# Gated expert tiles computed in turned form with biases as columns and their outputs scattered by token, and an opening without its own barrier

## What is computed

```python
D, H, E, K = 128, 342, 8, 2
d2 = sum(xs*xs) + sum(centroid*centroid) - 2 * xs @ centroid.T
w, sel = top_k(sqrt(max(d2, 1e-12)), K);  w = softmax(w)
for e in range(E):
    h = silu(xs @ Wg[e] + bg[e]) * (xs @ W1[e] + b1[e])
    out = out + we[:, e:e+1] * (h @ W2[e] + b2[e])
```

## Time and profile before

| | us |
|---|---|
| runs | 2288.75, 2294.0, 2300.62 (median 2294.0) |
| profiled execution, its own time | 2291.14 |
| its span | 2289.4 |
| PE busy in the span | 1860.5 (81%) |
| DVE, ACT, POOL busy | 1044.9, 846.4, 639.2 |
| mean granted TensorE clock | 0.887 |

### The profile page before, as it was taken

One profiled execution on the slowest core, in us unless ns is written; L12 is line 12 of the kernel. 1 busy time (PEld: TensorE's weight loads), 2 busy tenths in 40 slices (PEclk: granted clock), 3 DMA queues, 4 the chain that ended last, 5 costly groups with the idle time before them and its releaser, 6 DMA issues.

```text
span 2289.4 us, 47265 instructions
## 1 busy us (share of the span) xinstructions
PE 1860.5 (81%) x18716; PEld 1258.7 (55%) x18716; DVE 1044.9 (46%) x2763; ACT 846.4 (37%) x2360; POOL 639.2 (28%) x637
## 2 busy tenths in 40 slices
PE   3999984785699999799996029999207999999988
PEld 1555563664587788555555015555104666666773
DVE  4566556665421212356555102222234555555558
ACT  1333321664244444233332002222103555555636
POOL 4122103675110111212210560000571333333315
PEclk8999976887699999899997559999658999999979
DMA  4000000000000000200002140000111000000001
GB/s 150 12 12 7 2 1 23 19 6 5 1 1 2 2 1 1 88 12 12 7 2 86 39 117 19 19 20 19 39 43 53 6 6 6 6 6 1 1 1 38
DMA packets 47940, 51.11 MB, mean 22 GB/s; under 512 B 8025, under 2 KB 38633, under 8 KB 47465
## 3 DMA queue, kind: packets, MB, share of 16 engines
q1 hardware_dynamic: 43628, 39.64, 5.6%
q0 software_dynamic: 4096, 8.40, 1.3%
HBM read 32.25 MB, written 15.77 MB: 21 GB/s over the span
## 4 chain that ended last, share of the span: by engine, by line
PE 57%; issue 9%; POOL 9%; DVE 5%; POOLq 4%; DMA 1%; ACT 1%; DVEq 1%; SPq 0%; ACTq 0%
PE single L1471 5%; PE quad L1459 5%; PE quad L1783 4%; PE pair L362 3%; PE single L1802 3%; POOL arena L2034 3%; POOL tokens_by_tile L2024 3%; PE single L413 2%; PE quad L390 2%; PE pair L2190 2%; PE quad L2190 1%; PE pair L1418 1%; PE single L2202 1%; PE quad L2167 1%; PE quad L2216 1%
## 5 line engine op out<-in xcount | busy, mean ns | idle before, releaser
L531 DVE TENSOR_REDUCE arena<-pair 128x8 f32<-128x1024 f32 x128 | 156.8, 1225 | 156.5 <-PE pair L362 154.1
L2423 POOL TENSOR_TENSOR arena<-arena 128x512 f32<-128x512 f32 x128 | 130.4, 1040 | 310.3 <-DVE arena L2346 310.3
L613 POOL TENSOR_SCALAR arena<-arena 128x512 f32<-128x512 f32 x56 | 86.7, 1565 | 330.3 <-ACT arena L467 330.3
L1971 DVE TENSOR_TENSOR arena<-quad,arena 128x342 f32<-128x342 f32 x72 | 37.1, 515 | 273.7 <-ACT arena L1840 171.2
L238 POOL TENSOR_TENSOR rstd<-var_eps,neg_half 128x4 f32<-128x4 f32 (+1 forms) x64 | 65.6, 1024 | 333.5 <-DVE var_eps L234 237.8
L513 ACT ACTIVATE arena<-quad 128x1024 f32<-128x1024 f32 x128 | 124.2, 1022 | 69.5 <-PE quad L396 69.5
L1529 ACT ACTIVATE arena<-quad,arena 128x256 f32<-128x256 f32 x256 | 110.8, 475 | 101.8 <-PE quad L1459 101.8
L362 PE MATMUL pair<-arena 32*128 32x512 f32 x512 | 147.4, 653 | 0.0
L2034 POOL DMA_INDIRECT arena<-outputs_by_tile,arena x64 | 61.5, 960 | 277.0 <-DMA outputs_by_tile<-arena 258.5
L1459 PE MATMUL quad<-arena,wide 128*128 128x256 f32 x512 | 123.3, 389 | 4.6 <-issue 3.8
L2283 ACT ACTIVATE arena<-pair,arena 128x128 f32<-128x128 f32 x256 | 90.9, 380 | 90.7 <-DVE arena L2341 90.7
(11 more groups left out here) (475 smaller groups left out, 4410.6 us busy)
## 6 DMA issues: line engine op xcount, KB each, us to landing
arena<-in_ctxT SPq DMA_DIRECT2D x32, 256.0 KB, 2.8
tokens_by_tile<-arena SPq DMA_DIRECT2D x8, 576.0 KB, 6.6
arena<-tokens_by_tile SPq DMA_DIRECT2D x8, 576.0 KB, 7.7
outputs_by_tile<-arena SPq DMA_DIRECT2D x72, 64.0 KB, 1.5
wide<-in_w SPq DMA_DIRECT2D x2, 2048.0 KB, 9.7
wide<-in_wgu SPq DMA_DIRECT2D x1, 2736.0 KB
x<-in_x SPq DMA_DIRECT2D x4, 512.0 KB, 6.0
out_x<-x SPq DMA_DIRECT2D x8, 256.0 KB, 2.3
```

What stands on the lines that cost most here:

```text
L531: dve.tensor_reduce(mx[m % 2][:, 8 * p:8 * p + 8], S[:].rearrange("p (h k) -> p h k", h=8), AX.X, ALU.max).then_inc(s["s_free"], 1)
L613: mm = pool.tensor_scalar(kv[g % 2][:, :, a, :], kf[g % 2], kmask[:, a:a + 1], None, ALU.mult)
L2423: pool.tensor_tensor(part, part, inv[t % 3][:, 4 * r:4 * r + 4].unsqueeze(2).broadcast_to([P, 4, P]), ALU.mult).then_inc(s["norm_ready"], 1)
```

## The change

**Opening.** The load phase has no barrier. SP issues x part 0, the eight loads of the first attention, the first two context tiles, and then the rest. DVE computes the statistics of two groups, and those of group g+2 inside the attention at its batch 4g. POOL computes only the constants that this attention needs (`consts_in`), takes `rstd` group by group (`setup_r`), and makes the causal mask and `earlier` at g = 2. The masks of layer 2 are made by DVE at batch 7.

**Routing.** A row of the token table has 130 words: the token, its number, and its first choice. The row indices are ready before the list of experts by tile. The three-way split of the biases, its DRAM trip and its broadcast are gone; six small products with a one-hot list give `bcols`, the biases as columns for each tile. `W2` has a 115th row with its bias, which meets a row of ones in `hidT`.

**Tiles.** ACT copies the tile's 684 columns of weights from `wide` to `wt` (`copy_weights`), picked by a register of its own. PE uses pieces of 114 columns of `wt` as the stationary operand and the turned tokens as the moving one, so that the hidden layer comes out turned and needs no transposes. Silu takes the bias column on ACT, three pieces; DVE adds the other bias and multiplies, three pieces. DVE copies the turned tokens and the result. POOL scatters each tile's result to its token's row of `outputs_by_choice`, with an index list that DVE computes every 9 tiles (`places`); rows of padding have an index beyond the bound and are skipped.

**End.** SP waits for the last stores and loads two blocks of 256 KB per group, ACT scales them (8 instructions per group), POOL adds the two, DVE adds to x and takes the statistics.

```diff
@@ load_sync
+            tokens(0)
+            attention_weights(0)
+            first_ctx[0](sp)
+            for i in range(1, 4):
+                tokens(i)
+            attention_weights(2)
...
-            barrier(sp, 0)
@@ small_heads, vector
                 for n in range(N):
                     g, j = divmod(n, G)
+                    if l == 0 and j == 0 and g + 2 < NG:
+                        first_stats(dve, g + 2)
+                    if l == 0 and n == 7:
+                        later_masks(dve)
@@ gated_experts, sync
-                for n in range(TILES):
-                    sp.wait_ge(s["y_copied"], n + 1)
-                    sp.dma_start(done[n * P:(n + 1) * P], ysb[n % SLOTS]).then_inc(s[f"stored{n % SLOTS}"], 16)
+                for n in range(SLOTS):
+                    sp.wait_ge(s[f"stored{n}"], 16 * (TILES // SLOTS))
+                for g in range(NG):
+                    for i in range(2):
+                        rows = slice((i * B + g * G) * P, (i * B + g * G + G) * P)
+                        sp.dma_start(yg[:, i, g * G:g * G + G, :], done[rows].rearrange("(r p) d -> p r d", p=P)
+                                     ).then_inc(s[f"landed{g}"], 16)
@@ tensor
+                def first(n):
+                    pe.wait_ge(s["xgT_ready"], n + 1)
+                    pe.wait_ge(s["w_ready"], n + 1)
                     if n >= 2:
-                        pe.wait_ge(s["sg_ready"], n - 1)
-                        pe.wait_ge(s["hid_ready"], n - 1)
-                    for i in range(2):
-                        dst = bank[1 + 2 * i + n % 2][:, 0:F]
-                        pe.matmul(dst, pick[0:3, :], rows[0:3, ds(e * ROW + i * F, F)], start=True, stop=False)
-                        mm = pe.matmul(dst, xgT[n % 2], wide[:, ds(e * STEP + i * F, F)], start=False, stop=True)
+                        pe.wait_ge(s["sg_ready"], FB * (n - 1))
+                    for f in range(FB):
+                        mm = pe.matmul(g_bank[n % 2][0:FR, f * P:(f + 1) * P], wt[n % 2][:, f * FR:(f + 1) * FR],
+                                       xgT[n % 2], start=True, stop=True)
...
+                for n in range(-2, TILES):
...
-                        turn_hidden(n)
-                    if 0 <= n - 1 < TILES:
-                        second(n - 1, expert.pop(n - 1))
+                        second(n, pe.value_load(texp[0:1, n:n + 1], min_val=0, max_val=E - 1))
@@ scalar
+                def copy_weights(n):
+                    e = act.value_load(texp[0:1, n:n + 1], min_val=0, max_val=E - 1)
                     if n >= 2:
+                        act.wait_ge(s["u_ready"], n - 1)
+                    act.activation(wt[n % 2], wide[:, ds(e * STEP, 2 * F)], ACT.Copy).then_inc(s["w_ready"], 1)
@@ gpsimd
+                for n in range(TILES):
+                    pool.wait_ge(s["y_copied"], n + 1)
+                    pool.indirect_dma_start(done, bass.IndirectOffsetOnAxis(ap=back_i[:, n:n + 1], axis=0),
+                                            ysb[n % SLOTS], None, bounds_check=2 * B * P - 1, oob_is_err=False
+                                            ).then_inc(s[f"stored{n % SLOTS}"], 16)
+                    if n % 8 == 4 and n < 64:
+                        root(n // 8)
-                    for n in range(g * G, g * G + G):
-                        for i in range(2):
-                            pool.indirect_dma_start(yg[:, i, n, :], None, done,
+                    pool.wait_ge(s["y_scaled"], g + 1)
+                    pool.tensor_tensor(yg[:, 0, both, :], yg[:, 0, both, :], yg[:, 1, both, :], ALU.add
+                                       ).then_inc(s["y_added"], 1)
```

More of the change, by code:

```diff
@@ L216, in load_pool @@
             pool.drain()
-            pool.affine_select(out=earlier[:].rearrange("p (e f) -> p e f", e=E),
-                               in_=earlier[:].rearrange("p (e f) -> p e f", e=E), compare_op=ALU.is_gt, fill=0.0,
-                               base=0, pattern=[[1, E], [-1, E]], channel_multiplier=0)
-            for g in range(NG):
-                pool.wait_ge(setup_v, g + 1)
-                rstd_of(pool, g * G)
-            barrier(pool, 0)
         def stats_of(dve, first, bn, agg):
@@ L1849, in scalar @@
+                    act.wait_ge(s["g_ready"], n + 1)
+                    for f in range(FB):
+                        act.activation(sg[n % 2][0:FR, f, :], g_bank[n % 2][0:FR, f * P:(f + 1) * P], ACT.Silu,
+                                       bias=bcols[0:FR, f, n:n + 1]).then_inc(s["sg_ready"], 1)
+                for n in range(-2, TILES - 1):
                     if 0 <= n + 2 < TILES:
-                        copy_tile(n + 2)
+                        copy_weights(n + 2)
                     if 0 <= n + 1 < TILES:
@@ L1852, in scalar @@
                         gate(n + 1)
-                    if 0 <= n - 1 < TILES:
-                        copy_y(n - 1)
                 act.wait_ge(s["shifted_ready"], 1)
                 act.activation(gap, gap, ACT.Exp).then_inc(s["exp_ready"], 1)
+                act.wait_ge(s["weights_ready"], 1)
+                for g in range(NG):
+                    act.wait_ge(s[f"landed{g}"], 16 * 3)
+                    for i, w in ((0, w1st), (1, w2nd)):
+                        for j in range(G):
+                            n = g * G + j
+                            mm = act.activation(yg[:, i, n, :], yg[:, i, n, :], ACT.Copy, scale=w[:, n:n + 1])
+                    mm.then_inc(s["y_scaled"], 1)
@@ new lines, in copy_y @@
+                def copy_y(n):
+                    dve.wait_ge(s["y_ready"], n + 1)
+                    if n >= SLOTS:
+                        dve.wait_ge(s[f"stored{n % SLOTS}"], 16 * (n // SLOTS))
+                    dve.tensor_copy(ysb[n % SLOTS], y_bank[n % 2][:, 0:P]).then_inc(s["y_copied"], 1)
+                dve.wait_ge(s["ones_ready"], 1)
+                dve.wait_ge(s["bcols_copied"], 1)
+                for n in range(-2, TILES):
+                    if 0 <= n + 2 < TILES:
+                        if (n + 2) % PART == 0:
+                            places((n + 2) // PART)
+                        copy_tile(n + 2)
@@ L2451, in load_other @@
         def load_other(eng):
-            barrier(eng, 0)
+            pass
         phases.append((load_sync, load_other, load_other, load_dve, load_pool))
```

353 lines of the change are left out of this document (194 added, 159 removed).

## The result

| | before | after |
|---|---|---|
| median of 4 runs, us | 2294.51 | 2105.51 (2101.97 to 2113.96) |
| ratio | | 0.918, 95% interval 0.915 to 0.922 |
| span of the profiled run | 2289.4 | 2104.5 |

A forecast was written before the change was run, and what follows sets the result against it. Bounds taken: a transfer before the first attention, PE in the tile loop, POOL's issues around it. Opening 21, routing 1, tiles 71 and end 69 sum to 162 us less than 2294: 2132 us, range 2098 to 2175.

The forecast's parts named there:

- Opening, -21: Start to first scores: earlier context tiles and no barrier bring the first scores from 41.05 to 20 us, 21 less.
- Routing, -1: Routing, scatter and reload: indices come slightly earlier, scatters and reload keep their time; 1 us less, ends minus 2 to plus 4.
- Tiles, -71: Tile loop: PE stays the bound, a tile falls from 3.50 to 2.5 us, the loop from 260.8 to 190.
- the 9.6 assumed: Start of the tile loop: 8.8 us for filling and the first tiles, plus 0.8 for `places`.
- The trace decides for 0.128, which includes the switches between blocks: Tile loop on PE: a float32 row priced at the measured 0.128 us, not the skill's 0.112; a tile 2.51 us.
- PE's rows follow closer: Tile loop rival: rows without register operations follow closer, 2.2 us a tile, 22 less: 2110 (skill's gap 2105); chance 0.15.
- The rivals on ACT and POOL: Tile loop: ACT bounds a tile at about 3 us, 2168, chance 0.12; POOL's indexed store bounds it, 2312, chance 0.04.
- End, -69: Last product to the next phase: steps sum to 31.6 us against 101.0, 69 less.
- `rstd` and barrier 1.2: End of the phase: the last `rstd` and the barrier take 1.2 us.
- DVE 8 x (0.69 + 1.8) = 19.9: End of the phase: DVE's additions and statistics set the pace at 2.5 us a group, 19.9 for eight.
- The disturbance rival: DVE's statistics delay the maxima (11 us), or DVE and POOL alternate at the end (17 us): 2143 to 2160; chance 0.09.
- The first steps: End, ahead of DVE's groups: copy and signals 0.5, scatter 2.3, first loads 4.4, ACT 2.2, POOL's addition 1.1 us.

The follow-up runs named there:

- the run with 128 rows: The kernel before, with each bias product kept in bfloat16 but over 128 rows (ones by zeros) instead of 3, biases left out: 2230.32 us.
- the run with fixed experts: The kernel before, with the expert of tile n fixed as n // 9 when the program is written, no register picks on PE: 2295.27 us, ratio 1.000.

## Why the prediction was right, and where it was off

**Opening, -21 against -22.** Right in size, and right in that the context tiles' place behind everything and behind a barrier made them late; the place alone is enough for that, and how the gain divides between place and barrier was not run. `project_k` came at 11.18 (12 to 13 forecast), the scores at 19.07 (20). The first attention kept its length, so DVE's statistics lay in its waits for PE, as argued.

**Routing, -1 against +0.7.** The scatter kept its 1.27 us, and the first part landed after 4.35 us (4.4 before); so the 520-byte rows did not delay the first part.

**Tiles, -71 against -105.** PE was the bound and the count of rows was right. The step that failed is the price of a row: "The six rows with `W2` took 1507.90 - 1507.13 = 0.77 us to the next row, 0.128 each, and the turning 1504.61 - 1504.40 = 0.21". Both stretches touch a bias product of 3 rows, whose missing load-ahead put 0.10 us into each. Free of it six rows take 0.67 and the turning 0.11. 0.11 + 18 x 0.11 = 2.09, not 2.51: 30 us. The start of the loop took 4 us less than the 9.6 assumed. The Trainium skill's rule (TensorE: Matmul & The Clock Gate, Back-to-back issue gap), two passes of 55.8 ns, gave 0.112 a row and 2.12 a tile; the trace agrees (0.109 to 0.112). In the same section the Trainium skill calls this the gap of an isolated product and gives about 81 ns at 128 columns for a stream of weight loads and products; two of those would be 0.162 a row, and the trace does not agree with that, though each row has its own weight load. That a float32 row is two passes is borne out by the run with 128 rows: a bfloat16 row of 342 columns takes 0.15 us there (1433.62 to 1433.77), a float32 one 0.29. "The trace decides for 0.128, which includes the switches between blocks" was the wrong reading: the trace held a disturbance that the change removes. The rival *PE's rows follow closer* (0.15) is what happened, but its reason, register operations between the rows, is refuted by the run with fixed experts (0.77 for the six rows with `W2`, as before).

**The rivals on ACT and POOL.** ACT's copy took 780 ns (742 estimated), three silus 0.88 us back to back (0.83), POOL's store 0.98 (1.27, with the way to the next one; two in a row stand 1.29 apart); ACT was busy 112 of 157 us. Each silu with its pointer operand lasts 364 ns where a copy of the same columns had taken 277; the Trainium skill (ScalarE: Activation LUTs, What ACT_TABLE_LOAD costs) names 93 ns, and the 87 here agree. Three in a row take 0.88 us and not 3 x 0.364 = 1.09, so in the trace they overlap, and the price is 0.29 each.

**End, -69 against -60.** "`rstd` and barrier 1.2" was 7.0: the drain behind the indexed DMAs, 5.8 of the 9.4 us missed. It stood in the earlier trace rows as 6.42 <-POOLq and was passed over. "DVE 8 x (0.69 + 1.8) = 19.9" was 22.6, 2.7 more: seven held copies cost 3.5, and a group without one takes 2.34 instead of 2.49. The disturbance rival was there in kind (17 us bound), at a sixth of its size. The first steps were 11.3 instead of 10.5.

**Sum.** The tiles came 34 us under, the end 9 over, each other stretch within 2: 2132 against 2105.5. The time lies in the rival's band, 2098 to 2115 (0.15), and not in the forecast's own, 2115 to 2150 (0.60). That it lies in the stated range is in part luck: with the end as forecast, 9.4 us shorter, it would have been 2096, below 2098. The 2105 that the prediction works out by the Trainium skill's gap is met by the same luck: by it the loop would be 27 us shorter than forecast, it was 34 shorter, and the end gave 9 back.

## What to carry to other kernels

Before a product is priced by a row of the old trace, look at what stands next to that row: a neighbour that the change removes may sit in the price. A product with very few rows costs far more than its columns (here 0.41 us for 0.13 us of streaming, on average), so in a loop of full products biases are better put into a ones row of a wide product or into the operand of an activation. Before two errors of a sum are called small, look whether they cancel. Give the first transfers a kernel needs the first places in the queue, and put a drain behind a series of indexed DMAs where its engine has nothing to do.

## What was not expected of the hardware

- The first drain of POOL behind indexed DMAs ends about 6 us (5.97 and 5.99) after the instruction ahead of it, whether it stands right behind the last store or at the end of the phase. With one placed earlier, the one at the end is over 0.09 us after the last `rstd`.
- A product of 3 rows keeps both its own weight load and the next one from running ahead, in bfloat16 and in float32.
- With 3-row products in float32 the granted clock stayed at 0.50 for 500 us of unbroken PE work, where it was 1.00 with the bfloat16 ones. The cause is open.
- Beside an addition of POOL over 512 columns, DVE's copy of 4 columns takes 0.67 us instead of 0.17 and ends with the addition, while its four aggregations keep their 0.38 us together.
